# Projections and counts as pairs of row tiles over two periods, with both banks drained in one

## The reference, cut to what matters

```python
x = _layernorm(L0_attn_x)                      # 16 batches x 512 tokens x 256
x = x + attention(xn, Wq, Wk, Wv, Wo, qn_w, kn_w) + experts(xn, centroids, ln_g, ln_b, w1, b1, w2, b2)

# attention, per batch and head (16 heads of 16)
q = rms_norm(proj(Wq), qn_w); k = rms_norm(proj(Wk), kn_w); v = proj(Wv)
out = softmax(q @ k.T * scale) @ v @ Wo.T

# routing: each of 8 experts in turn takes its C = 1024 best tokens among those not yet taken
for e in range(E):
    s = jnp.where(taken, -jnp.inf, scores[:, e])
    _, idx = jax.lax.top_k(s, C)
```

## Time and profile before

| | us |
|---|---|
| median of 3 runs | 1099.46 |
| lowest and highest run | 1098.99, 1105.58 |
| the profiled execution | 1102.91 |
| its span, first to last instruction | 1101.2 |
| PE busy | 1047.7 |
| DVE busy | 821.6 |
| ACT busy | 745.3 |
| POOL busy | 715.7 |

### The profile page before, as it was taken

One profiled execution on the slowest core, in us unless ns is written; L12 is line 12 of the kernel. 1 busy time (PEld: TensorE's weight loads), 2 busy tenths in 40 slices (PEclk: granted clock), 3 DMA queues, 4 the chain that ended last, 5 costly groups with the idle time before them and its releaser, 6 DMA issues.

```text
span 1101.2 us, 20938 instructions
## 1 busy us (share of the span) xinstructions
PE 1047.7 (95%) x7222; PEld 678.5 (62%) x7222; DVE 821.6 (75%) x1856; ACT 745.3 (68%) x966; POOL 715.7 (65%) x754
## 2 busy tenths in 40 slices
PE   4799999899999999999999997999999999999997
PEld 3445555444444544544454442488998899998897
DVE  8799896587777778686877778686767776776861
ACT  3488888678888878888788885864536555455550
POOL 5577878566675766866766855646676566766334
PEclk9899999899999999999999999999999999999999
DMA  4867868458658668667675778233445243443313
GB/s 142 189 138 155 214 160 165 116 105 178 140 125 176 117 154 154 140 136 155 146 156 122 175 135 213 79 101 78 91 89 128 49 121 82 88 121 64 65 20 39
DMA packets 86361, 138.16 MB, mean 125 GB/s; under 512 B 12768, under 2 KB 38624, under 8 KB 86240
## 3 DMA queue, kind: packets, MB, share of 16 engines
q1 hardware_dynamic: 57392, 103.06, 41.6%
q0 software_dynamic: 12288, 16.79, 9.2%
q10 hardware_dynamic: 16560, 16.78, 5.9%
HBM read 86.25 MB, written 50.33 MB: 124 GB/s over the span
## 4 chain that ended last, share of the span: by engine, by line
PE 74%; DVE 9%; issue 6%; ACT 4%; POOL 3%; DMA 3%; SPq 1%; ACTq 0%; POOLq 0%; another core or an unknown queue 0%; DVEq 0%
PE W L1454 16%; PE S L1440 15%; PE pv L492 14%; PE S L477 11%; PE W L438 8%; PE W L449 4%; ACT prob L689 3%; PE W L463 2%; DMA stq<-parts 2%; SPq L323 1%; PE R L408 1%; DVE raw L819 1%; PE R L1426 1%; DVE xb L765 1%; PE pv L1426 1%
## 5 line engine op out<-in xcount | busy, mean ns | idle before, releaser
L689 ACT ACTIVATE prob<-S 128x1024 f32<-128x1024 f32 x512 | 498.4, 1022 | 118.6 <-PE S L477 117.4
L492 PE MATMUL pv<-prob,v 128*17 128x512 f32 x2048 | 248.6, 599 | 1.8 <-DVE oT L852 1.7
L477 PE MATMUL S<-stq,stk 64*128 64x512 f32 x1024 | 203.1, 461 | 17.9 <-ACT prob L689 9.1
L477 PEld LDWEIGHTS S<-stq,stk 64*128 64x128 f32 x1024 | 84.8, 186 | 149.9 <-ACT prob L689 111.0
L1716 POOL DMA_INDIRECT out<-prob,order_rows x64 | 105.8, 1653 | 48.0 <-DVE prob L1656 37.1
L1176 POOL TENSOR_TENSOR sq<-raw 128x512 f32<-128x512 f32 x62 | 64.4, 1040 | 87.0 <-DVE raw L819 56.8
L492 PEld LDWEIGHTS pv<-prob,v 128*17 128x17 f32 x2048 | 46.4, 96 | 118.0 <-issue 116.3
L1516 ACT ACTIVATE wq_act<-S,b 128x512 f32<-128x512 f32 x64 | 43.9, 687 | 94.7 <-PE S L1440 89.2
L1440 PE MATMUL S<-raw_nT,xT_w 128*128 128x512 f32 x384 | 91.1, 395 | 0.0
L1210 POOL TENSOR_TENSOR lo<-full,hi 128x512 fp32r<-128x512 f32 x62 | 80.0, 1290 | 5.0
L1440 PEld LDWEIGHTS S<-raw_nT,xT_w 128*128 128x128 f32 x384 | 71.6, 188 | 17.7 <-issue 1.7
(11 more groups left out here) (255 smaller groups left out, 2629.5 us busy)
## 6 DMA issues: line engine op xcount, KB each, us to landing
stk<-parts SPq DMA_DIRECT2D x192, 128.0 KB, 4.3
stq<-parts SPq DMA_DIRECT2D x192, 128.0 KB, 6.4
xT<-in_w SPq DMA_DIRECT2D x32, 512.0 KB
parts<-hi SPq DMA_DIRECT2D x63, 256.0 KB, 2.1
parts<-lo SPq DMA_DIRECT2D x63, 256.0 KB, 2.0
out<-ao ACTq DMA_DIRECT2D x32, 256.0 KB, 4.7
xb<-in_x ACTq DMA_DIRECT2D x13, 512.0 KB, 5.3
xb<-in_x SPq DMA_DIRECT2D x2, 512.0 KB, 5.1
```

The source lines that it names most:

```text
L477: ins = e.matmul(S[n % 2][:, h, :], stack["k"][u][64 * h:64 * h + 64, p, c * P:(c + 1) * P], stack["q"][u][64 * h:64 * h + 64, p, :], star ...
L492: ins = e.matmul(pv[32 * j:32 * j + VW, :], v[b % 2][:, c, 8 * u + 4 * g + j, :], prob[(2 * t + j // 2) % RING][:, j % 2, :], start=(c == ...
L689: e.activation(prob[n % RING][:, :, :], S[n % 2][:, :, :], ACT.Exp).then_inc(s_exp, 1)
```

## The change

All projections inside the periods, and the search's counts in most periods, go from the full array to its two row tiles of 64 rows, the tiles that the scores use. A row tile takes half of the contraction, so each matmul becomes two, one per tile. They are issued as a pair that writes W[0] and W[1]: in the first half row tile 0 works for group 0 and row tile 1 for group 1, in the second half the two swap, and both banks are complete at the end of the second.

- q and k: six pairs of 512 columns in each of two periods, behind h3.
- v and the output: in each of two periods one 128-token column block of both groups, six pairs of 256 columns between h2 and h3 (first turn) and six behind h3 (second turn). The second turn waits for the first on new semaphores (`s_vp_turn`, `s_wo_turn`).
- The counts (steps 1 to 10 of an expert, and the first step of the first): one matmul in row tile 0 before the last pair or the last two, one in row tile 1 behind them, which waits for the first on `r_lower`. At an expert's step 0 (from the second on) and step 11 they stay in the full array, behind the projection.
- DVE drains both banks at the head of its period, before the search: q/k u = 0 at place 0, u = 1 at place 2, v at place 4. ACT copies both output banks at place 6, one before exponential 0 and one behind exponential 1; the two transfers out go to places 7 and 0.
- POOL squares both halves in the period of the drain.
- The projections of batch 0 and u = 0 of batch 1, before the periods, and the last batch's output stay as they were.

```diff
-def qk_at(nb, i):
-    return PERIODS * (nb - 2) + 6 + i if i < 2 else PERIODS * (nb - 1) + i - 2
+def qk_at(nb, u):
+    return PERIODS * (nb - 1) + (1 if u else -1)
...
-def v_at(nb, i):
-    return PERIODS * (nb - 1) + 2 + i
+def v_at(nb):
+    return PERIODS * (nb - 1) + 3
...
+    def project_qk_steps(e, nb, u, half, steps):
+        if half == 0 and steps[0] == 0:
+            e.wait_ge(s_xl, 2 * nb + 2)
+            if u:
+                e.wait_ge(s_raw, 4 * nb + 2)
+            elif nb >= 3:
+                e.wait_ge(s_ao, 2 * (nb - 3) + 2)
+            else:
+                e.wait_ge(s_v, 2 * (nb - 1) + 2)
+        for j in steps:
+            d, (pw, px) = j // 3, PRODUCTS[j % 3]
+            for r, g in ((0, half), (1, 1 - half)):
+                rows = slice(64 * r, 64 * r + 64)
+                ins = e.matmul(W[g][:, :], w["qk"[g]][pw][rows, d, u * P:(u + 1) * P], (xh, xl)[px][nb % 2][rows, d, :],
+                               start=(half == 0 and j == 0), stop=(half == 1 and j == 5))
+        if half and steps[-1] == 5:
+            ins.then_inc(s_proj, 2)
...
+    def project_v_steps(e, nb, c, turn, steps):
+        if turn == 0 and c == 0:
+            e.wait_ge(s_xl, 2 * nb + 2)
+            e.wait_ge(s_raw, 4 * nb + 4)
+        elif turn and steps[0] == 0:
+            e.wait_ge(s_vp_turn, 2 * (nb - 1) + c + 1)
+        for j in steps:
+            d, (px, pw) = j // 3, PRODUCTS[j % 3]
+            for r, g in ((0, turn), (1, 1 - turn)):
+                rows, at = slice(64 * r, 64 * r + 64), (2 * g + c) * P
+                ins = e.matmul(W[g][:, c * D:(c + 1) * D], (xh, xl)[px][nb % 2][rows, d, at:at + P], w["v"][pw][rows, d, :],
+                               start=(turn == 0 and j == 0), stop=(turn == 1 and j == 5))
+        if turn == 0:
+            ins.then_inc(s_vp_turn, 1)
+        elif c and steps[-1] == 5:
+            ins.then_inc(s_vp, 2)
...
+    def route_tensor(e, ex, i, r=None):
+        rows = slice(0, P) if r is None else slice(64 * r, 64 * r + 64)
+        last = r != 0
+        if r == 1:
+            e.wait_ge(r_lower, lower(ex, i))
...
+        def sums(to, what, of):
+            return e.matmul(to, what[rows, :], of[rows, :], start=(r != 1), stop=last)
...
@@ tensor_program
-                heads(e, b, 4 * kk + 3)
...
+                ex, i = routed(at)
+                route = ex is not None and (ex < E - 1 or i == 0)
+                by_tiles = route and (0 < i < STEPS or ex == 0 and i == 0)
+                half = kk % 2
+                if kk in (0, 1) and nb < B:
+                    heads(e, b, 4 * kk + 3)
+                    project_qk_steps(e, nb, 1, half, range(0, 5))
+                    if by_tiles:
+                        route_tensor(e, ex, i, 0)
+                    project_qk_steps(e, nb, 1, half, range(5, 6))
+                elif kk in (2, 3) and nb < B:
+                    project_v_steps(e, nb, half, 0, range(0, 6))
+                    heads(e, b, 4 * kk + 3)
+                    project_v_steps(e, nb, half, 1, range(0, 4))
+                    if by_tiles:
+                        route_tensor(e, ex, i, 0)
+                    project_v_steps(e, nb, half, 1, range(4, 6))
...
@@ scalar_program
-                if b and kk in (5, 6):
-                    evict_o(e, b - 1, kk - 5)
+                if b and kk == 6:
+                    evict_o(e, b - 1, 0)
                 softmax(e, 4 * at)
...
                 softmax(e, 4 * at + 1)
-                if b and kk in (5, 6):
-                    put_out(e, b - 1, kk - 5)
+                if b and kk == 6:
+                    evict_o(e, b - 1, 1)
+                if b >= 2 and kk == 0:
+                    put_out(e, b - 2, 1)
+                if b and kk == 7:
+                    put_out(e, b - 1, 0)
...
@@ vector_program
+                for m, u in ((nb, 0), (nb, 1)):
+                    if m < B and qk_at(m, u) + 1 == at:
+                        if at:
+                            turn_raw(e, m, 2 * u)
+                        turn_raw(e, m, 2 * u + 1)
+                if nb < B and v_at(nb) + 1 == at:
+                    copy_v(e, nb, 0)
+                    copy_v(e, nb, 1)
                 ex, i = routed(at)
```

More of the change, by code:

```diff
@@ new lines, in project_o_steps @@
+    def project_o_steps(e, b, c, turn, steps):
+        if turn == 0 and c == 0:
+            e.wait_ge(s_onl, 2 * b + 2)
+            if b + 2 < B:
+                e.wait_ge(s_v, 2 * (b + 2) + 2)
+            else:
+                e.wait_ge(s_ao, 2 * b)
+        elif turn and steps[0] == 0:
+            e.wait_ge(s_wo_turn, 2 * b + c + 1)
+        for j in steps:
+            u, (px, pw) = j // 3, PRODUCTS[j % 3]
+            for r, g in ((0, turn), (1, 1 - turn)):
+                rows, at = slice(64 * r, 64 * r + 64), (2 * g + c) * P
+                ins = e.matmul(W[g][:, c * D:(c + 1) * D], (onh, onl)[px][rows, u, at:at + P], w["o"][pw][rows, u, :],
+                               start=(turn == 0 and j == 0), stop=(turn == 1 and j == 5))
+        if turn == 0:
+            ins.then_inc(s_wo_turn, 1)
+        elif c and steps[-1] == 5:
+            ins.then_inc(s_wo, 2)
@@ L1090, in vector_program @@
                     place_rest(e)
-                for m in (nb, nb + 1):
-                    for i in range(4):
-                        if m < B and qk_at(m, i) + 1 == at:
-                            turn_raw(e, m, i)
                 if scored(at) is not None:
@@ L1104, in vector_program @@
                         sum_squares(e, nb, u)
-                for i in range(2):
-                    if nb < B and v_at(nb, i) + 1 == at:
-                        copy_v(e, nb, i)
                 if b and kk == 1:
@@ L1259, in gpsimd_program @@
                     second_power(e, scored(at - 1))
[L1260 to L1263 removed]
+                for m, u in ((nb, 0), (nb, 1)):
+                    if m < B and qk_at(m, u) + 1 == at:
+                        if at:
+                            square(e, m, 2 * u)
+                        square(e, m, 2 * u + 1)
                 if b and kk == 0:
```

76 lines of the change are left out of this document (41 added, 35 removed).

## The result

The changed kernel takes 1107.12 us (median of 20 runs, 1103.92 to 1110.4), the kernel before 1101.99 us on the same chips (20 runs, 1098.99 to 1105.58): a ratio of 1.005 with a 95% interval of 1.0041 to 1.006. It is 5 us slower. The prediction said 1100.4 us against a median of 1099.5, "the same", with a range of 1088 to 1114.

What follows compares the result with a forecast made beforehand. The prediction took a loop through ACT's exponentials (4.81 us), equal to PE's own sum (4.82), as the bound. Terms from -2.1 to +3.8 us summed to +0.9: 1099.5 + 0.9 = 1100.4 us, range 1088 to 1114.

Steps and rivals of the forecast that it cites:

- periods 0 to 31: Before the search: second turn's wait +0.9, place 2 -1.1, place 6 +0.4, POOL's queue from period 28 +1.1 us.
- periods 32 and 33: Where DVE splits the scores: two drains first, less contention, no wait for the transposed output; +0.4 us.
- starts at place 4: Expert starts in periods 44, 68, 92: search starts later, POOL's work comes earlier; -1.3 us, bounds -2 and +4.
- starts at place 0: Expert starts in periods 56, 80, 104: DVE's search ends at 5.4, not 4.2; 5.75 against 4.82, +3.8 us.
- waits for the q stack: PE's waits in periods 63 and 111, 1.05 us each, go because POOL's squares come earlier; -2.1 us to 0.
- The loop decides, not PE: In the search, the loop through ACT's exponentials lasts 4.81 us, PE's sum 4.82; shorter projections make PE wait longer.
- the signs I named: If right: PE busy some 92%, score loads' wait for ACT up 20 to 30 us, DVE's head waits gone.
- PE's sums: PE's work a search period: 4.35 to 4.77 us with q/k, 4.7 (4.4 to 5.1) with v or output projections.
- rival B: The v and output pairs cost more than a full matmul; from 0.03 a pair +12, 1113 us; chance 0.15.
- Place 2 and place 6: Search periods 2 and 6 of each batch of eight, counted from 0: 5.13 becomes 4.84 us, 5.11 becomes 5.20.
- Drains at the head: DVE does both drains, 1.4 us, before the search: nothing in ordinary periods, +3.8 and -1.3 us at expert starts.
- Rival C: In ordinary even search periods DVE misses the count, 31 periods at 0.3: +9, 1110 us; chance 0.09.

Runs made afterwards that it cites:

- the run with fewer products: Kernel before, with the projections of later batches making 3 of their 6 products: 1090.23 us, ratio 0.9894.
- those with short exponentials: Exponentials of periods 40 to 117 over 384 of 512 columns: kernel before 1097.39 us, ratio 0.9953; changed kernel 1099.19 us, ratio 0.9961.
- The run with full counts: Changed kernel with each count as one matmul of the full array behind the projection: 1104.3 us, ratio 1.0023.
- the short square: Changed kernel with POOL's second square of each drained pair over 64 of 512 columns from batch 1 on: 1100.41 us, ratio 0.997.
- the kernel with single drains: Kernel before with each drain and copy, still one to a period, at the head of DVE's period: 1097.12 us, ratio 0.9956.
- the first run of that group: Changed kernel with DVE's drains and copies back in their old places, behind the search: 1140.44 us, ratio 1.0348.
- the run with another order: Changed kernel with the second of POOL's two squares at the end of its period: 1100.97 us, ratio 1.0029.

## Why the prediction came out as it did

The time was inside the range and the kind was right, but the sum was +0.9 where +3.7 is read in the periods and +5.1 in the medians. (Of the 6.7 us from 1100.4 to 1107.1, another 2.5 are the starting point: the median of the kernel before was 1099.46 over 3 runs and is 1101.99 over 20.) A range of 26 us asks little of a sum this small, and the sum's errors partly cancel. By its terms, in us:

| term | predicted | in the profiles |
|---|---|---|
| periods 0 to 31 | +1.3 | +4.0 |
| periods 32 and 33 | +0.4 | +1.6 |
| starts at place 4 | -1.3 | -1.4 |
| starts at place 0, with the two periods behind them | +2.8 | +1.5 |
| waits for the q stack (63, 111) | -2.1 | -2.1 |
| the other periods from 34 to 117 | -0.7 | +0.8 |
| from 118 on | +0.5 | -0.8 |

(The prediction has +3.8 and -1.7 in the fourth and sixth row: 1.0 of the +3.8 takes back a gain of place 2 that the -1.7 counts for all batches. Here each period stands in one row.) Two of the measured numbers are flattered by the clock in the profile of before: +1.6 would be +3.2 and -0.8 would be +0.2.

**The loop decides, not PE.** Right. Batch 6 was forecast at 38.99 and is 39.04; the run with fewer products and those with short exponentials show it directly. Three of the signs I named were no use: PE's busy share did not fall to 92%, since the modelled ends of its matmuls fill each wait (4.85 of 4.85 at place 5 with loads waiting for ACT), the wait for ACT grew by 11 us, not by 20 to 30, and DVE's waits for PE at the head of its period are not gone: its drains wait 39.9 us for projections, 21.7 before, and its `answer` 38.5 for the counts, 66.5 before.

**PE's sums and the pairs (rival B).** Right: pairs of 256 columns are 0.12 apart, h3 follows h2 by 1.05 (forecast 1.06), the turn's wait is at most 0.2, two counts cost 0.08 and not 0.2. PE's sums, 4.5 and 4.6, stand against 4.55 and 4.7, in part by luck: no row stood behind the 0.55 for h0 and h1, which took 0.64 to 0.66 where they did not wait, and the cheap counts make up for it. Missing in the sum was the gap at the end of place 3 or 7 (from h1 to h1 5.04 to 5.16 for 4.84, and 4.84 to 4.95 for 4.81), some 2 us in all; the other periods of the search are 1.5 above the forecast in all. The run with full counts shows that it comes with the counts in the tiles.

**Place 2 and place 6.** From h1 to h1, as the loop was summed, place 2 is 4.84 (forecast 4.84) and place 6 5.26 (5.20). The mechanism given for place 2, the inverse rms between the exponentials, is shown by the version that moves it.

**Drains at the head.** "Ends at 5.4 and not 4.2": period 56 is 5.80 (forecast 5.75). But "the place-2 gain is lost there too" was wrong: period 58 is 4.86. And the -1.3 at place 4 was right only as a sum. It is a gain of 4.9, which the head brings, and a loss of 3.5. Of that loss the short square takes back 2.2 and the full counts 1.1. The second copy's share was not run by itself; in the trace of period 44 DVE's two copies take 1.29 us, where the one copy of the kernel with single drains takes 0.69. I had weighed the head as a cost with a small relief, when it was the only part of the change that makes the kernel faster.

**The step that failed** is the one on the periods before the search, with its like for 32 and 33: +1.3 and +0.4, where +4.0 and +1.6 (+3.2 with the kernel before at full clock) were measured. It priced the turn's wait, place 2 and place 6 and, for period 28 alone, POOL's queue. What it left at nothing is of three kinds.

- Periods 11 and 19, +1.3 in all. Two squares in one period move the scaling 1 us back onto the normalization. The trace of before had it: POOL with one square between its power and its scaling, and DVE's normalization fitted into what POOL leaves. The short square takes 1.2 of it back.
- Periods 5 and 6, +2.2 in all. The two copies of v put the moments and all behind them 1.4 later (with the copies behind them, in the first run of that group, period 5 is 5.85 instead of 6.85), and the clock adds to period 6. The short square takes 1.5 back here.
- Periods 15 and 23, +1.3 in all. There it is neither: the next h0 waits for the q stack, 0.57 and 0.69 us (132.37 and 178.11 in the trace), which is all of both. So waits like the two that the prediction rightly had as gone (63 and 111) appear elsewhere. The row for the changed kernel, of which 5.0 is again the wait at the start:

```profile
PE S L547 <- DMA stq<-parts: 6.2, 3, 5.0
```

The last transfer into the stack took 8.0 us from issue to landing here and 6.7 in the profile of before, and it varies between profiles of one program: of four with the program of before up to there, one has such a wait (0.54, in the run with another order), and of four with the changed one all do (1.26, 1.7, 0.6 and 1.5 us in both places together). So the change seems to make it more frequent, but one pair of profiles is no measure of it. What lengthens the transfer stays open.

**Rival C** happened, though not where I put it: the loads of the counts wait for DVE 16.3 us instead of 5.9, in period 32 and at the starts and not in ordinary periods. That the expert starts suffer more from counts in tiles is shown by the run with full counts.

What stays open is how often the clock falls in periods 33 and 122. The +5.1 of the medians lies between the +3.7 of the two profiles and the 6.3 with the kernel before at full clock in both; one execution of each kernel cannot settle it.

## What to carry to other kernels

When two engines run in step, find the loop before pricing the work. Take half of the supposed bottleneck's work out in one run, and if a fifth of it comes back, the rest of the tuning is elsewhere. When two small jobs are merged into one period, follow each of their consumers through every queue, most of all through an engine that shares its port with the one that is late. And take a change apart even if it comes out near zero: here a part worth 5 us was hidden under a rest that cost 10.

## What the runs showed of the hardware that I had not expected

- A matmul of 7 columns in one row tile, put between the pairs, costs its own tile 0.04 us and the other nothing (0.11 and a switch in the full array). But ahead of a flag test the next scores come 0.36 behind it, where a count in the full array has 0.11.
- One more change from scores to weighing and back costs 0.29 us (3.49 against 3.20).
- Where PE stood for 2.3 of 6.9 us, the next period ran at a granted clock of 0.75. The profile of before has a low clock too, from 230.60 on in period 33 (first row). The run with fewer products has the same program there, kept a clock of 1.00 and took 5.30 us for the whole period, instead of 6.87 (second row):

```profile
230.60:235.93 5.33, 5.33 (x27) 2.14 (x19) 3.70 (x6) 2.88 (x4) 3.47 (x5) 0.68 1.08 143
```

```profile
229.32:234.62 5.30, 4.83 (x32) 2.16 (x31) 5.16 (x11) 3.66 (x4) 3.93 (x5) 1.00 1.08 139
```

Of a difference of 1.6 us in a single profile none may be laid to a change before the clock's row has been read.
